# A perceiver layer on one core: the opening of self attention moved into the last tile of cross attention

## The reference, cut to what matters

```python
x = x + xattn(layernorm(x), ctx, seg)      # 16 heads, key window of 9 around seg
x = x + attn(layernorm(x))                 # 16 heads of 16, causal, 64 tokens
x = x + ffn(layernorm(x))                  # 8 experts, top 2, and 2 shared experts

def attn(x):                               # x: (16, 64, 256)
    q, k, v = x @ Wq, x @ Wk, x @ Wv
    s = einsum(q, k) * tril                # the mask multiplies
    return einsum(softmax(s / 8), v) @ Wo

def xattn(q, kv, seg):                     # latent attention
    kv_c, q_c = kv @ W_kvc, q @ W_dq
    s = (q_nope . k_nope + rope(q_r) . rope(k_r)) * scale
    s = where(seg - 8 <= key <= seg, s, -1e30)
    return (softmax(s) @ v) @ W_o
```

## Time and profile before

| what | value |
|---|---|
| median of three runs | 560.95 us (557.5 to 562.01) |
| the profiled execution | 562.37 us, its span 560.6 us |
| PE matmul busy | 532.9 us, 95% of the span |
| DVE, ACT, POOL busy | 48%, 29%, 10% |
| share of PE in the chain that ended last | 86% |
| mean granted TensorE clock | 0.982 |
| last tile of cross attention, first scores to last projection's end | 175.55 to 197.22 us |
| first transpose of self attention's probabilities | 212.5 us |

### The profile page before, as it was taken

The page is one execution under the profiler, slowest core; times in us unless marked ns, Lnnn a source line. Parts: engine busy times, 40 slices in busy tenths (PEclk is TensorE's granted clock), DMA queues, the critical chain, the costliest instruction groups (busy, mean ns, idle before and its releaser), DMA issues.

```text
span 560.6 us, 11604 instructions
## 1 busy us (share of the span) xinstructions
PE 532.9 (95%) x4468; PEld 390.0 (70%) x4468; DVE 268.3 (48%) x573; ACT 162.4 (29%) x306; POOL 58.8 (10%) x70
## 2 busy tenths in 40 slices
PE   7979999999999989998699999999999999999996
PEld 6667787787888878886477777555555555556774
DVE  3547767767776357888444222122222222222244
ACT  1244434534444315444221111122211221121111
POOL 2000000000000013122102341000000000000450
PEclk9699999999999999999889999999999999999999
DMA  9600000000594076000252115468888778761231
GB/s 302 258 0 20 20 1 19 19 1 18 177 396 196 2 307 261 2 0 1 69 214 76 49 56 212 157 215 289 306 280 284 270 289 311 268 215 63 66 104 66
DMA packets 24457, 82.06 MB, mean 146 GB/s; under 512 B 2881, under 2 KB 16513, under 8 KB 20322
## 3 DMA queue, kind: packets, MB, share of 16 engines
q1 hardware_dynamic: 21536, 75.93, 37.2%
q0 software_dynamic: 1536, 4.20, 2.3%
q10 hardware_dynamic: 1346, 1.38, 0.8%
HBM read 73.11 MB, written 8.39 MB: 145 GB/s over the span
## 4 chain that ended last, share of the span: by engine, by line
PE 86%; DVE 5%; issue 4%; DMA 2%; ACT 1%; POOL 0%; SPq 0%; DVEq 0%; POOLq 0%
PE ps L1626 16%; PE ps L1585 13%; PE ps L1192 11%; PE ps L1653 8%; PE ps L1613 6%; PE ps L1226 5%; PE ps L1245 5%; PE ps L1270 5%; PE ps L1258 3%; PE ps L1463 3%; DMA w_routed<-in_w_qr 2%; PE ps L1241 1%; PE ps L1218 1%; PE ps L1511 1%; DVE w_routed L588 1%
## 5 line engine op out<-in xcount | busy, mean ns | idle before, releaser
L1626 PE MATMUL ps<-w_routed,xnT 128*64 x320 | 93.8, 436 | 0.6 <-issue 0.6
L1585 PE MATMUL ps<-w_shared,xT_all 128*128 128x384 f32 (+1 forms) x256 | 76.6, 444 | 0.0
L1160 ACT COPY hidT<-ps 128x384 f32<-128x384 f32 x36 | 17.2, 479 | 181.0 <-PE ps L1192 176.1
L1626 PEld LDWEIGHTS ps<-w_routed,xnT 128*64 128x64 f32 x320 | 42.0, 137 | 37.4 <-issue 26.1
L1585 PEld LDWEIGHTS ps<-w_shared,xT_all 128*128 128x128 f32 x256 | 48.2, 195 | 18.0 <-issue 2.8
L889 DVE COPY hidT<-ps 128x256 f32<-128x256 f32 x36 | 15.3, 424 | 92.9 <-PE ps L1192 90.2
L1192 PE MATMUL ps<-consts_a,w_routed 128*128 128x128 f32 x400 | 51.7, 275 | 6.2 <-ACT w_routed L1012 2.9
L1192 PEld LDWEIGHTS ps<-consts_a,w_routed 128*128 128x128 f32 x400 | 44.5, 141 | 13.5 <-issue 4.6
L1653 PE MATMUL ps<-w_routed,hidT 128*64 x200 | 47.4, 384 | 0.0
L1626 PE MATMUL ps<-w_shared,xnT 128*64 128x384 f32 (+1 forms) x160 | 46.9, 436 | 0.0
L1626 PE MATMUL ps<-x_up,xnT 128*64 128x384 f32 (+1 forms) x160 | 46.9, 436 | 0.0
(11 more groups left out here) (175 smaller groups left out, 879.4 us busy)
## 6 DMA issues: line engine op xcount, KB each, us to landing
w_routed<-in_w_routed SPq DMA_DIRECT2D x8, 1920.0 KB, 14.1
x_up<-in_w_routed SPq DMA_DIRECT2D x10, 1280.0 KB, 5.7
w_shared<-in_w_routed SPq DMA_DIRECT2D x10, 1280.0 KB, 6.0
b_down<-in_w_routed SPq DMA_DIRECT2D x10, 640.0 KB, 5.5
w_shared<-in_w_routed SPq DMA_DIRECT2D x10, 640.0 KB, 4.9
w_shared<-in_w_shared SPq DMA_DIRECT2D x1, 3840.0 KB, 12.1
w_shared<-in_w_uvo SPq DMA_DIRECT2D x1, 2560.0 KB, 15.5
x_slots<-sil SPq DMA_DIRECT2D x16, 160.0 KB, 2.2
```

The lines of the kernel that those rows point to most:

```text
L1160: act.copy(hidT[:, 0:3, :], ps[:, 4, 0:CA].rearrange("p (c t) -> p c t", t=P)).then_inc(hT_a, 1)
L1585: last = pe.matmul(ps[:, b, 0:hi - lo], xT_all[:, i, k, :], w[:, at:at + hi - lo], start=k == 0, stop=k == KT - 1)
L1626: last = pe.matmul(ps[rows, b, 0:hi - lo], xnT[:, k, rows], w, start=k == 0, stop=k == KT - 1)
```

## The change

The opening of self attention is no longer a block of its own. Each engine has a `last_body` for tile 7 in which the opening's steps stand between those of the tile, where the fillers were. `normed(0)` waits only for the fourth value of L467 and `normed(1)` for the sixth. All fillers (`keep_busy`) are gone. `general` stands behind the whole, and if its branch is taken, the opening is done once more from the x of that path (`g_again`). SP's loads of experts 4 to 7 wait also for `bon`, the first divided values of self attention. `b_values(0)` now waits for `x2_done`, since it writes the banks that the last projection used. Moved functions keep their instructions.

```diff
         def general(eng, tile, again=None):
             eng.wait_ge(far_ready, 1)
             flag = eng.value_load(far_i[0:1, 0:1], min_val=0, max_val=2)
             with eng.If(flag > 0):
...
+                eng.wait_ge(bmax, 1)
                 with eng.Fori(0, NT) as i:
                     tile(i)
+                if again is not None:
+                    again()
+                eng.wait_ge(g_step, ALL_STEPS)
...
             sp.wait_ge(x2_done, NT)
             sp.wait_ge(win_ready, 1)
+            sp.wait_ge(bon, 1)
             for e in range(E // 2, E):
                 sp.dma_start(w_routed[:, e, :], dram["w_routed"][e]).then_inc(late_in, 16)
```

On DVE:

```diff
+            def last_body(i, link_):
+                normed(0, 4, xn, bT_ps, bxn, 0)
+                softmax_in(i, 0, link_)
+                residual(i - 1, link_)
+                softmax_in(i, 1, link_)
+                normed(1, 6, xn, bT_ps, bxn, 1)
+                b_queries(0)
+                values_out(i, 0, link_)
+                b_maximum(0)
+                values_out(i, 1, link_)
+                b_queries(1)
...
-            body(NT - 1, link, False, True, False)
+            dve.wait_ge(moe_in, 16)
+            last_body(NT - 1, link)
             residual(NT - 1, link)
...
-            normed(0, 2 * NT, xn, bT_ps, bxn, 0)
-            normed(1, 2 * NT, xn, bT_ps, bxn, 1)
-            b_queries(0)
-            b_maximum(0)
-            b_queries(1)
             b_body(0, link, True, True, False)
```

On ACT:

```diff
+            def last_body(i):
+                exps(i, 0)
+                b_xT_out(0)
+                pt_out(i, 0)
+                exps(i, 1)
+                b_k_out(0)
+                b_v_out(0, 0)
+                pt_out(i, 1)
+                b_xT_out(1)
+                ut_out(i, 0)
+                ut_out(i, 1)
+                b_k_out(1)
+                b_v_out(1, 1)
```

On PE:

```diff
+            def last_body(i):
+                scores(i, 0)
+                project(i - 1)
+                pe.wait_ge(aw_in, 16)
+                b_transposes(0, None)
+                probs_T(i, 0)
+                scores(i, 1)
+                b_qkv(0)
+                values(i, 0)
+                b_transposes(1, None)
+                probs_T(i, 1)
+                b_scores(0)
+                values_T(i, 0)
+                values(i, 1)
+                b_q(1)
+                values_T(i, 1)
+                b_kv(1)
+                project(i)
...
-            body(NT - 1, False, True)
-            keep_busy(2)
-            project(NT - 1)
+            last_body(NT - 1)
...
-            general(pe, g_tile)
-            keep_busy(12)
+            general(pe, g_tile, g_again)
...
             def b_values(i, parity):
+                if isinstance(i, int) and i == 0:
+                    pe.wait_ge(x2_done, NT)
                 pe.wait_ge(bpt_done, i + 1)
```

More of the change, by code:

```diff
@@ L729, in g_tile, with g_again @@
                 stage.end(dve.tensor_scalar(rstd[:, bass.ds(i, 1)], g_rstd[:], 0.0, None, ALU.add))
[L731 to L751, removed]
+            def g_again():
+                for t in range(2):
+                    stage = Stage(dve, "AGAIN", f"norm{t}", NT)
+                    stage.end(dve.tensor_scalar(xn[:], x_sb[:, t, :], mv[:, t, 0:1], rstd[:, t:t + 1], ALU.subtract, ALU.mult))
+                    stage = Stage(dve, "AGAIN", f"qm{t}", NT)
+                    stage.end(b_queries_work())
+                stage = Stage(dve, "AGAIN", "max", NT)
+                stage.step(b_masked())
+                stage.end(b_top())
+            general(dve, g_tile, g_again)
             def values_of(rows):
@@ L1080, in g_tile, with g_again @@
                 stage.end(last)
[L1082 to L1088, removed]
+            def g_again():
+                for t in range(2):
+                    for name, work in ((f"x{t}", b_x_work), (f"k{t}", b_k_work)):
+                        stage = Stage(act, "AGAIN", name, NT)
+                        stage.end(work())
+                    stage = Stage(act, "AGAIN", f"v{t}", NT)
+                    stage.end(b_v_work(t))
+            general(act, g_tile, g_again)
             def b_OT_out(i):
@@ L1093, in b_OT_out @@
                          ps[:, 2, D:2 * D].rearrange("p (b h q) -> p b h q", b=TB, h=2)).then_inc(bot_done, 1)
[L1095 to L1104, removed]
-                                    ps[rows, 3, D:2 * D].rearrange("p (h c) -> p h c", c=2 * DH))
-                last.then_inc(bv_done, 1)
             def b_exp(i):
@@ L1197, in keep_warm @@
                     pe.matmul(bank(7, cols=2 * P), zeros[:, 0:P], zeros[:, 0:2 * P], start=True, stop=True)
-            def keep_busy(n):
-                for _ in range(n):
-                    pe.matmul(ps[:, 3, 0:P], ident[:], ident[:], start=True, stop=True)
             def xT_work():
@@ L1335, in project, with b_x_work, b_transposes @@
                 project_work().then_inc(proj_ps, 1)
+            def b_x_work():
+                for k in range(KT):
+                    last = transpose(ps[:, 2, k * P:(k + 1) * P], xn[:, k * P:(k + 1) * P])
+                return last
+            def b_transposes(x, o):
+                if o is not None:
+                    pe.wait_ge(bon, o + 1)
+                    for b in range(TB):
+                        last = transpose(ps[:, 2, D + b * P:D + (b + 1) * P], On[:, b])
+                if x is not None:
+                    pe.wait_ge(bxn, x + 1)
+                    after(pe, bqm, x)
+                    last = b_x_work()
+                last.then_inc(bT_ps, 1)
@@ new lines, in tall, with b_q_work, b_kv_work @@
+            def tall(w, b):
+                for g in range(KT):
+                    for k in range(KT):
+                        last = pe.matmul(ps[:, b, g * P:(g + 1) * P], w[:, k, g * P:(g + 1) * P], xnT[:, k, :],
+                                         start=k == 0, stop=k == KT - 1)
+                return last
+            def b_q_work():
+                return tall(a_wq, 2)
+            def b_kv_work():
+                tall(a_wk, 3)
+                for k in range(KT):
+                    last = pe.matmul(ps[:, 3, D:2 * D], xnT[:, k, :], a_wv[:, k, :], start=k == 0, stop=k == KT - 1)
+                return last
@@ new lines, in b_scores @@
+            def b_scores(i):
+                pe.wait_ge(bk_done, i + 1)
+                pe.wait_ge(bqm, i + 1)
+                after(pe, bs_used, i)
+                b_scores_work().then_inc(bs_ps, 1)
+            def last_body(i):
[16 more added lines that the diff above has]
+                project(i)
```

155 lines of the change are left out of this document (86 added, 69 removed).

## The result

| | median, us | lowest to highest | runs |
|---|---|---|---|
| before | 560.88 | 557.5 to 563.34 | 21 |
| changed | 558.67 | 553.88 to 562.86 | 20 of 21 |

The ratio is 0.9942, 95% interval 0.9922 to 0.9963: 3.25 us, or 0.58%, faster. Forecast were 557.9 us, a gain of 3.1, and a time within 1%. The ratio leaves out three slower executions of the changed kernel, one of 890.24 us at a mean granted clock of 0.558 (left out of the table as well) and two of 562.5 and 562.86 us at 0.970; the two medians of the table differ by only 2.21 us. All rows of "after" are from one execution of 559.91 us, span 556.9.

A forecast was written before the change was run, and what follows sets the result against it. PE is 95% busy, but the seam hangs on the chain of waits to self attention's first exponential. That comes 4.7 us earlier, less 1.6 for the clock: 3.1 off 560.95, so 557.9 us; range 554.0 to 561.5.

The forecast's parts named there:

- The last tile: Cross attention's tile 7, taking in the opening's work: its last projection would end at 201.2, 4.0 us later than before.
- both gaps: New PE idle times in tile 7: 0.2 us before tile 1's transposes, 0.85 us before the second divided values' transposes.
- The jam: Rival: DVE's waits in tile 7 cost 2 us more than forecast; gain 1.1 to 2.7, 558.3 to 559.9 us; chance 0.11.
- POOL's price: POOL's flag and branch before its subtraction: 1.60 us from its last power's start, subtraction at 204.55, exponential 4.7 us earlier.
- more than that: Rival: POOL at its lower bound (5.7 us) and low stretch from 268.3 moved into idle time; 553.7 to 555.3; chance 0.20.
- "The other readers of the flag are covered by this": Behind the branch: PE has scores (1.5 us) and two transposes meanwhile, DVE's next normed x is ready at 204.9; no added cost.
- The clock: Thin PE stretch behind the last projection: granted clock falls to 0.50 for 3.2 us, better than even odds, costing 1.6 us.
- The sum: Whole kernel: 4.7 us gained at the seam less 1.6 for the clock, 3.1 us, so 557.9 us; chance 0.40.
- "I let the gain stand to the end": Behind the seam: a chain of the same steps, so the forecast gain of 3.1 us would last to the end.
- The late weights: SP's four expert loads, moved behind the first division: taking them from the opening costed at nothing, up to 0.5 us gain possible.
- The cover: Late expert loads land at about 233, well before self attention's end (before at 276.41): some 40 us to spare.
- "Slower, since the clock stays low without fillers": Rival: low clock from the projection's end through self attention's first steps; 563.0 us, 564.7 with POOL's upper bound; chance 0.07.

The follow-up runs named there:

- the reordered kernel: Changed kernel with tile 0's subtraction and exponential ahead of the flag, and PE's first self-attention step doing normed-x-dependent work last; 555.23 us against 561.62 before, ratio 0.9876.

## Why the prediction came out right, by its steps

- **The last tile: 4.0 us later forecast, 3.50 measured** (the last power 19.34 behind A, before 15.84). The walk held, with both gaps; the waits in it were a little shorter (0.29 and 0.66 for 0.2 and 0.85). The jam did not come.
- **POOL's price: 1.60 from the start of its power taken, 1.12 measured** (204.18 to 205.30), which is 0.57 after its end, where I had said 1.05. I had taken DVE's row as the nearest; POOL, with two operations to pass over, is cheaper. With the 0.5 us of the tile the exponential came 5.67 us earlier and not 4.7, so of the rival "more than that" this half came true. So, in the profiled execution, did the other: the low stretch from 268.3 is gone, and POOL's last power of self attention comes 4.48 earlier from A, where the one before it comes 3.29 earlier.
- **"The other readers of the flag are covered by this": this step failed.** I let DVE's price stand at 1.60, from a branch whose body the change itself lengthens. It is 3.97 (1.58 without the repeat), and DVE's normed x, not the exponential, released PE. It cost little only because the exponential was hardly earlier: the probabilities' transposes start 1.64 us after the exponential does, before 1.34, so 0.3 us.
- **The clock: a fall forecast at better than even odds, price 1.6.** It fell, at 206.7. From the transposes to the mark it is 6.91 us now and 4.82 before, 2.1 of price. From the seam on the two profiles hold about as much of the low level: before it lay at 268.3 to 271.5 and 278.2 to 285.4, now at 206.7 to 213.5 and 285.2 to 288.6. The row from 35 to 38, which the prediction set against a fall, was no evidence: in the profile after, the same stretch of the same code is followed by the low clock.
- **The sum**: 5.67 less 0.3 less 2.1 is 3.28 at the mark; 3.1 was forecast. Errors of 1.0 us one way (tile and POOL) and 0.8 the other (clock and DVE) cancelled. The number was right partly by luck. So was its agreement with the whole time: "I let the gain stand to the end" did not hold in the profiled pair, where 2.1 us more were gained behind the seam, and 1.7 lost ahead of A and 1.2 outside the span.
- **The late weights: costed at nothing. This term failed too.** I looked at whether DVE's and PE's pieces grew beside the loads, and they did not. I did not ask what else goes through the DMA queues. Without the added wait the gain at the mark is 0.21 us. My sum came out only because it held neither the longer stall nor its cure. The cover was real: the loads start at 217.17, 9.9 us behind the exponential for the 7 forecast, and none of PE's waits after 290 is for a DMA.
- **"Slower, since the clock stays low without fillers"** was the right mechanism for the kernel before (7.4 us at the mark). In the changed kernel the tile's real work stands in for them, and only the seam stays thin.

Still open: whether an instruction transfer is the whole of each stall, and whether its price grows with the body or comes in one step, which two lengths can't tell. PE's own 1.60 us amid its scores, gone without the flag, is of the same kind, and no run took it away by itself.

## What to carry to other kernels

A branch whose body never runs is not free. Here its price on DVE rose with a longer body and again with bulk loads in the DMA queues, which together took back nearly all that moving work across it gained; issuing those loads after all engines were past it gave that back. Ask of a thin stretch not which fillers to put in but which real work needs only what is ready already: here such an order, with an earlier exponential, gained twice what the change did, and fillers put back gained nothing. A fall of the clock seen once in a profile, or not seen, is one draw: look at the same stretch in a second profile before arguing from it. Before placing anything at a wait, look up which wait ends last there; two of these experiments missed because the first instruction behind it waited for another engine than the one I had in mind.

## What the runs showed of the hardware that was not expected

- Reading the flag and passing over the branch's body took DVE 1.58 us from the piece ahead to the piece behind, 3.97 with 12 more vector operations and their waits in the body, and 7.14 beside loads at a DMA share of 1.00. POOL took 0.57 us behind its power in the last two, with the loads and without.
- DVE's normed x reads and writes SBUF alone and takes 0.41 us. When it starts while POOL subtracts in SBUF it ends with POOL: started 0.07 us after POOL it took 1.98, started 0.23 after 1.82, and both ended 0.15 us after POOL's end (204.91 and 206.97). DVE pieces that read PSUM were not held (in the reordered kernel, masked queries 1.65 for four from 209.09 on, while POOL subtracted from 209.25). "GPSIMD Engine Reference" of the Trainium skill, in section "1. Specifications", says that POOL shares its SBUF interfaces with VectorE and contends with instructions that use two ports or two SBUF inputs. These rows agree that the two contend, and not by which of the two conditions; that both pieces end 0.15 us behind POOL's, whenever they started, looks like being held rather than slowed.
- The same thin stretch of the same code (35 to 38 us, PE busy 0.13 and 0.23 of 3 us) left the granted clock at 1.00 in the profile before and was followed by 0.53 in the one after.
